# Per-sample 128x128 mix with residual: x loaded as 4096 B rows by channel instead of 8192 B rows, products over 128 rows instead of two groups of 64, weights loaded plain

## The reference, cut to what matters

```python
def reference(x, itok, weights):          # x [128, 128, 1024], itok [128], weights [8, 128, 128]
    w = weights[itok]                     # one 128x128 matrix per sample
    return x + einsum('bct,bcd->bdt', x, w)
```

## Time and profile before

| | before |
|---|---|
| median of 3 runs | 323.73 us |
| the profiled execution, its own time | 324.45 us |
| its span, first to last instruction | 322.8 us |
| mean granted TensorE clock | 0.929 of 2.4 GHz |
| PE, DVE, ACT, POOL busy | 76%, 50%, 41%, 17% |
| DMA | 134.80 MB, mean 418 GB/s |
| load queue (SP), store queue (ACT) | 49.9% and 49.2% of 16 engines' span |

### The profile page before, as it was taken

One profiled execution on the slowest core, in us unless ns is written; L12 is line 12 of the kernel. 1 busy time (PEld: TensorE's weight loads), 2 busy tenths in 40 slices (PEclk: granted clock), 3 DMA queues, 4 the chain that ended last, 5 costly groups with the idle time before them and its releaser, 6 DMA issues.

```text
span 322.8 us, 3365 instructions
## 1 busy us (share of the span) xinstructions
PE 243.8 (76%) x1088; PEld 110.6 (34%) x1088; DVE 160.5 (50%) x131; ACT 133.8 (41%) x132; POOL 55.1 (17%) x140
## 2 busy tenths in 40 slices
PE   3489999999978766888966687868798666878300
PEld 3334444444643322334322233323343222333100
DVE  0417677676674535452646643555536356435500
ACT  1015565566663424443534432434624244324300
POOL 5041222221221111110101111111101011100000
PEclk9879999999999998997999997989979999979855
DMA  7999999999999999999999999999999999999994
GB/s 289 425 420 420 404 429 424 426 428 425 427 428 426 428 427 428 429 425 429 427 427 427 428 427 426 429 426 427 428 426 428 428 426 427 428 426 428 427 428 208
DMA packets 17558, 134.80 MB, mean 418 GB/s; under 512 B 1041, under 2 KB 1042, under 8 KB 1170
## 3 DMA queue, kind: packets, MB, share of 16 engines
q1 hardware_dynamic: 8848, 67.64, 49.9%
q10 hardware_dynamic: 8706, 67.11, 49.2%
HBM read 67.63 MB, written 67.11 MB: 417 GB/s over the span
## 4 chain that ended last, share of the span: by engine, by line
DMA 60%; PE 27%; issue 2%; DVE 2%; POOL 1%; DVEq 1%; POOLq 0%; ACTq 0%; SPq 0%
DMA out<-ring 39%; PE products L170 25%; DMA ring<-x 21%; PE products L149 2%; DVE ring L198 1%; POOL pick L108 1%; DVEq L41 1%; DVE table L186 1%; POOL selected L133 0%; POOLq L128 0%; POOL ones L101 0%; DVE pick L182 0%; DVEq L193 0%; SPq L96 0%; ACTq L222 0%
## 5 line engine op out<-in xcount | busy, mean ns | idle before, releaser
L170 PE MATMUL products<-ring,selected 64*128 64x512 f32 x1024 | 237.2, 617 | 52.5 <-DMA ring<-x 46.6
L198 DVE COPY ring<-products 64x1024 f32<-64x1024 f32 x128 | 156.4, 1222 | 132.1 <-PE products L170 130.1
L214 ACT COPY ring<-products 64x1024 f32<-64x1024 f32 x128 | 128.7, 1006 | 163.3 <-PE products L170 161.6
L170 PEld LDWEIGHTS products<-ring,selected 64*128 64x128 f32 x1024 | 105.1, 195 | 184.3 <-issue 115.3
L133 POOL COPY selected<-table 64x256 f32 x128 | 50.7, 396 | 226.5 <-PE products L170 197.7
L149 PE MATMUL products<-loaded,pick 32*128 32x256 f32 x64 | 6.5, 588 | 4.9 <-DVE pick L182 4.9
L214 ACT ACT_TABLE_LOAD x4 | 5.1, 1283 | 6.0 <-DVE ring L198 2.9
L149 PEld LDWEIGHTS products<-loaded,pick 32*128 32x128 f32 x64 | 5.5, 310 | 5.5 <-POOL pick L108 4.8
L186 DVE TENSOR_TENSOR table<-products,unit 128x1024 f32<-128x1024 f32 x2 | 3.7, 1928 | 6.8 <-PE products L149 6.8
L108 POOL TENSOR_SCALAR_AFFINE_SELECT pick<-ones 32x512 f32<-32x512 f32 x4 | 2.6, 658 | 0.3
L182 DVE COPY pick<-pick 128x512 f32<-128x512 f32 x1 | 0.4, 426 | 4.3 <-POOL pick L108 4.3
## 6 DMA issues: line engine op xcount, KB each, us to landing
ring<-x SPq DMA_DIRECT2D x32, 2048.0 KB, 23.1
out<-ring ACTq DMA_DIRECT2D x32, 2048.0 KB, 43.7
loaded<-weights SPq DMA_DIRECT2D x1, 512.0 KB, 3.6
subject_row<-subjects ACTq DMA_DIRECT2D x1, 0.5 KB
```

Of the source, the lines that this page charges most:

```text
L170: last = nc.tensor.matmul(products[:, b, g, n * BANK:(n + 1) * BANK], selected[part, k, e * mixed:(e + 1) * mixed], ring[part, s, e * time ...
L198: nc.vector.tensor_copy(ring[0:HALF, s, b * times:(b + 1) * times], products[b * HALF:(b + 1) * HALF, s % PSUM_BUFS, 0, :]).then_inc(even_ ...
L214: nc.scalar.copy(ring[HALF:channels, s, b * times:(b + 1) * times], products[b * HALF:(b + 1) * HALF, s % PSUM_BUFS, 1, :]).then_inc(odd_d ...
```

## The change

Loads take x by channel: partition c holds channel c, with 4096 B (1024 times) of sample 0 and then of sample 1 of each tile. A span's load of 2 MB therefore is 128 partitions by four rows of 4096 B, where it was 128 by two rows of 8192 B; in x the four rows of a partition lie 512 KiB apart. Stores stay as they are. A product takes all 128 channels at once: 4 products of 128 rows by 512 columns per tile, without accumulation, where there were 8 of 64 rows. POOL still copies one matrix per sample, now on 128 partitions by 128 columns (64 by 256 before). The weights are loaded as eight 512 B rows per partition instead of one 4096 B row; `pick`, its doubling and the spreading products go away, and one DVE instruction adds the unit matrix straight to the loaded weights.

```diff
-    x_rows = x.rearrange("b (q e) t -> (b q) (e t)", e=2).rearrange("(t p) f -> p t f", p=channels)
+    x_rows = x.rearrange("b c t -> c b t")
...
-            sp.dma_start(loaded[:], weights.rearrange("n (h l) d -> (n h) (l d)", l=SIDE)).then_inc(weights_loaded, DMA)
+            sp.dma_start(loaded[:], weights.rearrange("n c d -> c n d")).then_inc(weights_loaded, DMA)
             for s in range(0, TILES_PER_TURN, SPAN):
-                sp.dma_start(ring[:, s:s + SPAN], x_rows[:, s:s + SPAN, :]).then_inc(x_loaded[s // SPAN], DMA)
+                sp.dma_start(ring[:, s:s + SPAN].rearrange("c s (g t) -> c (s g) t", g=2), x_rows[:, 2 * s:2 * (s + SPAN), :]).then_inc(x_loaded[s // SPAN], DMA)
...
-            for j in range(quarters):
...
-                nc.gpsimd.affine_select(pick[part, :, :, 0, :], ones[part, :], [[1, pairs], [-HALF, 2], [-1, HALF]],
-                                        ALU.is_equal, 0.0, base=0, channel_multiplier=4).then_inc(pick_ready, 1)
...
+            nc.gpsimd.affine_select(unit[:], ones[:], [[-1, mixed]],
+                                    ALU.is_equal, 0.0, base=0, channel_multiplier=1).then_inc(unit_ready, 1)
...
-                        nc.gpsimd.tensor_copy(selected[part, k:k + 1, :],
-                                              table[part, bass.ds(subject, 1), :]).then_inc(weights_selected[s], 1)
+                        nc.gpsimd.tensor_copy(selected[:, k, g:g + 1, :],
+                                              table[:, bass.ds(subject, 1), :]).then_inc(weights_selected[s], 1)
...
-            for n in range(2):
-                for r in range(pairs):
-                    for j in range(quarters):
...
-                        last = nc.tensor.matmul(
-                            weights_by_pair[:, at:at + wide],
-                            pick[part, r, n].rearrange("p g q -> p (g q)"),
-                            loaded[part, r * wide:(r + 1) * wide],
-                            start=(r == 0), stop=(r == pairs - 1))
...
-                    for n in range(banks):
-                        for e in range(2):
-                            for g in range(2):
...
-                                last = nc.tensor.matmul(
-                                    products[:, b, g, n * BANK:(n + 1) * BANK],
-                                    selected[part, k, e * mixed:(e + 1) * mixed],
-                                    ring[part, s, e * times + n * BANK:e * times + (n + 1) * BANK],
-                                    start=(e == 0), stop=(e == 1))
+                    for g in range(2):
...
+                        pe.wait_ge((even_drained, odd_drained)[g][last_user], 2 * turn + 2)
+                        for n in range(banks):
+                            last = nc.tensor.matmul(
+                                products[:, b, g, n * BANK:(n + 1) * BANK], selected[:, k, g, :],
+                                ring[:, s, g * times + n * BANK:g * times + (n + 1) * BANK],
+                                start=True, stop=True)
...
-            nc.vector.tensor_copy(pick[:, :, :, 1, :], pick[:, :, :, 0, :]).then_inc(pick_doubled, 1)
-            dve.wait_ge(unit_ready, 2)
-            dve.wait_ge(weights_spread, 1)
-            for e in range(2):
-                nc.vector.tensor_tensor(
...
+            dve.wait_ge(unit_ready, 1)
+            dve.wait_ge(weights_loaded, DMA)
+            nc.vector.tensor_tensor(
+                table[:].rearrange("p n (b m) -> p n m b", b=2),
+                loaded[:].rearrange("p n (m b) -> p n m b", b=2),
+                unit[:].rearrange("p (m b) -> p m b", b=2).unsqueeze(1).to_broadcast([channels, n_subjects, HALF, 2]),
+                ALU.add).then_inc(table_ready, 1)
```

More of the change, by code:

```diff
@@ L17 @@
 HALF = 64
-QUARTER = 32
-SIDE = 8
 def subject_mix_kernel(nc: bass.Bass, x: bass.AP, subjects: bass.AP, weights: bass.AP, out: bass.AP):
@@ L46, in subject_mix_kernel @@
         ring = ctx.enter_context(nc.sbuf_tensor("ring", [channels, TILES_PER_TURN, row], F32))
[L48 to L55, removed]
+        loaded = ctx.enter_context(nc.sbuf_tensor("loaded", [channels, n_subjects, mixed], F32))
+        table = ctx.enter_context(nc.sbuf_tensor("table", [channels, n_subjects, mixed], F32))
+        ones = ctx.enter_context(nc.sbuf_tensor("ones", [channels, mixed], F32))
+        unit = ctx.enter_context(nc.sbuf_tensor("unit", [channels, mixed], F32))
+        selected = ctx.enter_context(nc.sbuf_tensor("selected", [channels, SELECT_BUFS, 2, mixed], F32))
         subject_row = ctx.enter_context(nc.sbuf_tensor("subject_row", [1, samples], I32))
         products = ctx.enter_context(nc.psum_tensor("products", [mixed, PSUM_BUFS, 2, times], F32))
-        weights_by_pair = products[:, 0].rearrange("p g t -> p (g t)")
         subjects_loaded = sem("subjects_loaded")
@@ L95, in _ @@
                     sp.wait_ge(stored[s // SPAN], turn * DMA + DMA)
-                    sp.dma_start(ring[:, s:s + SPAN], x_rows[:, bass.ds(tile + TILES_PER_TURN, SPAN), :]
+                    sp.dma_start(ring[:, s:s + SPAN].rearrange("c s (g t) -> c (s g) t", g=2), x_rows[:, bass.ds(2 * tile + 2 * TILES_PER_TURN, 2 * SPAN), :]
                                  ).then_inc(x_loaded[s // SPAN], DMA)
@@ L102, in _ @@
             pool.wait_ge(ones_ready, 1)
-            for j in range(quarters):
-                part = slice(j * QUARTER, (j + 1) * QUARTER)
-                if j:
-                    pool.wait_ge(pick_ready, j)
-                nc.gpsimd.affine_select(pick[part, :, :, 0, :], ones[part, :], [[1, pairs], [-HALF, 2], [-1, HALF]],
-                                        ALU.is_equal, 0.0, base=0, channel_multiplier=4).then_inc(pick_ready, 1)
-            pool.wait_ge(pick_ready, quarters)
-            for g in range(2):
[L112 to L117, removed]
+            nc.gpsimd.affine_select(unit[:], ones[:], [[-1, mixed]],
+                                    ALU.is_equal, 0.0, base=0, channel_multiplier=1).then_inc(unit_ready, 1)
             pool.wait_ge(subjects_loaded, DMA)
-            pool.wait_ge(table_ready, 2)
+            pool.wait_ge(table_ready, 1)
             with pool.Fori(0, turns) as turn:
@@ L125, in _ @@
                     for g in range(2):
-                        part = slice(g * HALF, (g + 1) * HALF)
                         subject = pool.value_load(subject_row[0:1, bass.ds(2 * tile + g, 1)]).with_bounds(
@@ L139, in _ @@
                 pe.sem_inc(product_ready[s], 1)
-            pe.wait_ge(pick_ready, quarters)
-            pe.wait_ge(pick_doubled, 1)
-            pe.wait_ge(weights_loaded, DMA)
-            for n in range(2):
-                for r in range(pairs):
-                    for j in range(quarters):
-                        part = slice(j * QUARTER, (j + 1) * QUARTER)
-                        at = j * BANK + n * wide
-                        last = nc.tensor.matmul(
-                            weights_by_pair[:, at:at + wide],
-                            pick[part, r, n].rearrange("p g q -> p (g q)"),
-                            loaded[part, r * wide:(r + 1) * wide],
-                            start=(r == 0), stop=(r == pairs - 1))
-            last.then_inc(weights_spread, 1)
             with pe.Fori(0, turns) as turn:
@@ L180, in _ @@
                 dve.sem_inc(even_drained[s], 2)
-            dve.wait_ge(pick_ready, quarters)
-            nc.vector.tensor_copy(pick[:, :, :, 1, :], pick[:, :, :, 0, :]).then_inc(pick_doubled, 1)
-            dve.wait_ge(unit_ready, 2)
-            dve.wait_ge(weights_spread, 1)
-            for e in range(2):
-                nc.vector.tensor_tensor(
[L187 to L191, removed]
+            dve.wait_ge(unit_ready, 1)
[5 more added lines that the diff above has]
+                ALU.add).then_inc(table_ready, 1)
             with dve.Fori(0, turns) as turn:
```

7 lines of the change are left out of this document (removed).

## The result

The changed kernel takes 330.73 us (median of 4 runs, 329.85 to 334.93) against 323.79 us; the ratio is 1.0197, 95% interval 1.0177 to 1.0216. Six more runs of the same kernel, made later (experiment 6), gave 329.78 to 336.70 us, ratio 1.0252 (1.0206 to 1.0298): the kernel spreads by itself, and experiment 6 shows where. Each of the two ratios leaves out its slowest run, 334.93 and 336.70 us, as disturbed; whether it was, or had the late end of experiment 6, is not shown. The profiled execution took 330.01 us, its span is 328.3 us.

What follows compares the result with a forecast made beforehand. The prediction took the DMA engines, full from 5 to 318 us, as the bound. Packets 3.6, weights 0.4 and the end 6.0 made +10.0 us, 333.7 us against 323.73; own range 330.5 to 337, overall range 327.0 to 341.0.

Steps and rivals of the forecast that it cites:

- The bound: Whole kernel: bytes and packets over the DMA engines' rate, plus a start and a short end; PE has slack.
- Turns by packet: Engines alternate queues by packet, so stores get 283 GB/s, loads 141, and no line of stores forms; chance 0.60.
- The packets: Load queue: 8192 packets become 16384 of half size, +3.6 us; weights as 512 B rows, +0.4 us.
- the 7 ns for a packet: DMA engines: time a packet costs beside its bytes, giving +3.6 us for 8192 added load packets.
- The upper bound of 24.5 ns: Load packets: extra time per 8192 B, from the weights' 4096 B packets, making 12.5 us.
- The end: After the last load: 5.0 us of idle DMA plus 1.0 us for a lone store's start, +6.0 us.
- The sum: Whole kernel: +10.0 us on the profiled execution, median 333.7 us against 323.73.
- At no cost: Products at 7.14 us per span, copies, queues and waits: all taken as costing nothing.
- bytes: Rival at the DMA queues: turns by bytes keep the line of stores, only packets cost, 327.7 us; chance 0.20.
- pitch: Rival in the loads: rows 512 KiB apart in x read slower than their packets, 342.6 us; chance 0.11.
- PE: Rival in the products: unhidden weight loads make PE the bound, 10.1 us per span, about 342 us; chance 0.03.
- merged packets: Rival in the load queue: neighbouring 4096 B rows taken as one packet, not slower, 323.3 us; chance 0.06.

Runs made afterwards that it cites:

- experiment 6: The changed kernel, unchanged, run again: 333.66 us, ratio 1.0252; profiled execution 333.71 us.
- experiment 7: Changed kernel with PE held back until the third span of x has landed: 333.58 us, ratio 1.0254.
- experiment 9: Kernel before with half the ring, 8 tiles per turn instead of 16: 336.83 us, ratio 1.0406.
- Experiments 3: Kernel before with loads alone in 4096 B packets, both halves of a row in turn, one DMA per tile: 335.01 us, ratio 1.0296.
- experiment 4: Kernel before with stores alone in 4096 B packets, both halves of a row in turn: 326.08 us, ratio 1.0055.
- experiment 1: Changed kernel with its stores split too, so both queues move 4096 B packets: 328.26 us, ratio 1.0131.
- experiment 5: Loads and stores on one queue: changed kernel 328.19 us, ratio 1.0126; kernel before 325.64 us, ratio 1.0050.
- experiment 2: Kernel before, each load or each store split into two DMAs of half rows: loads 340.65 us, 1.0513; stores 341.48 us, 1.0533 (in the order told).

## Why the prediction was right, point by point

**The bound**, right: the DMA is full until 294 us in both kernels, and a PE that starts 7 us earlier gains nothing (in experiment 7 a start 10 us later costs nothing that shows), because the ring covers it (with half the ring, experiment 9, the start costs 8.4 us).

**Turns by packet**, right, and the heart of it: 430 packets against 431, a store landing in 11.8 us (about 10 was forecast). Experiments 3 and 4 turn it round by giving the same small packets to one queue or the other: +9.6 or +1.8 us. A load landed in 43.3 us, not 60.

**The packets** were the term that was mis-sized: 3.6 + 0.4 = 4.0 us, where the runs have 1.8 (experiment 4), 2.4 (from the rate in experiment 1) and 2.5 (the pair of experiment 5, with layout, weights and products in it). The failed step is the 7 ns for a packet, taken from a difference of record lengths in the earlier trace rows; both queues at 4096 B give 4.7 ns. The whole loss until 294 us is 3.2 us; of it 23 x (423 - 411)/428 = 0.6 us lie in the stretch from 5 to 28 us, in which loads run mostly alone. The upper bound of 24.5 ns from the earlier trace rows was, as suspected, a start-up stretch.

**The end** was forecast as 6.0 us and is two things: 2.3 us in the first profile, 6.0 us in that of experiment 6. The step that failed is "its own load landed one period earlier": in the first profile the last two loads landed 5.6 us apart. The loads do not land evenly. PE and ACT's queue from 62 us on show how they come:

```profile
65.54 23.54 PE L123 MATMUL products<-ring,selected 128*128 128x512 f32 x48 [4.21 <-DMA ring<-x]
91.73 8.66 PE L123 MATMUL products<-ring,selected 128*128 128x512 f32 x16 [2.66 <-DMA ring<-x]
...
78.08 0.38 ACTq L170 DMA_DIRECT2D out<-ring  x1
84.94 0.38 ACTq L170 DMA_DIRECT2D out<-ring  x1
91.81 0.38 ACTq L170 DMA_DIRECT2D out<-ring  x1
103.12 0.38 ACTq L170 DMA_DIRECT2D out<-ring  x1
```

48 instructions are three spans in one run. Their stores follow each other by 6.9 us, less than the 7.4 us that each was forecast to take beside loads, so loads crawl (1.73 MB in the 12 us shown above); then the stores run out, loads have the DMA alone, and the next spans land close together. Where the last span falls in such a group goes with the end: with its neighbour (2.3 us) or alone (6.0 us). That this grouping chooses the ending is read from profiles of both kinds, not forced by a run.

The rows of the two ends say more. In experiment 6 the last store is issued 3.7 us later (325.14 against 321.44). Of these 0.9 us are a later start of span 31 (305.59 against 304.71). Another 1.8 us are its products, 8.83 us against half of 14.00: PE had been without products for 4.19 us, and the granted clock from 306 to 312 us was 0.72 of 2.4 GHz, part of that time at the lower level of 1.2 GHz; in the first profile PE had paused for 0.54 us, and the clock was 1.00 from 304.7 to 311.7 us. A further 0.84 us are the wait for the last load's latest part. The prediction had slow first products only in its upper bound (1.4 us), and had nothing for a late part of a load. Where its 6.0 us agree with experiment 6, luck has a part: it had the DMA idle in one stretch, between the last two stores, and there it idles ahead of span 31's store as well. The 1.0 us for the start of a lone store was right: by the trace its first packet comes 0.9 us after its issue (321.44 and 322.35).

**The sum**: 333.7 us was forecast; 330.73 us in the first runs, 333.66 us in the second. The first lie 3 us below the forecast, near the lower end of its own range (330.5 to 337). That the second meet it within 0.1 us is partly luck: their profile has 3.2 us until 294 us, where 4.0 were forecast for the packets and the weights, and 6.0 us after it.

**At no cost**, right: a span's products take 7.1 us (14.0 for two) with 128 rows, weight loads hidden; POOL's copies 293 ns. SP is held, the median issue of a reload taking 9.9 us, and ACT's issues stay at 0.38 us. Of the rivals, bytes, pitch, PE and merged packets are each ruled out by a row above (430 packets against 431; 411 and 423 GB/s without the pitch; 66.1 us of PE idle, all for loads; 17936 packets of the load queue).

## What to carry to other kernels

Where two DMA queues share the engines, look at the packets each has, not at the bytes: a queue whose packets are made smaller falls behind, and the line of waiting work moves to its side. Ask on which side a line is useful: in front of the last stores it hides the last computation, in front of the loads it hides nothing at the end. If loads must have small rows, put loads and stores on one queue or give stores rows of the same size (328.2 and 328.3 us here, against 330.7 and 333.7), and keep the ring deep enough for the start.

## What the runs showed of the hardware that was not expected

- An added packet is cheap (4.7 ns, 2.4 us for 8192), but its queue's share is not: the same packets cost +1.8 us on the store queue and +9.6 us on the load queue.
- The parts of one DMA do not land together: half of the last load's marks were there by 307.8 and 307.9 us in the two profiles of the changed kernel, the last one at 310.3 and at 315.2.
- 4096 B loads alone run at 410 GB/s, beside stores both together at 427. All packets from 116 to 122 us in the changed kernel, loads only:

```profile
DMA packets 617, 2.46 MB, mean 410 GB/s; under 512 B 16, under 2 KB 16, under 8 KB 617
```

- Half rows: taking every other 4096 B in one DMA and the rest in the next costs 16 to 17 us (experiment 2), in stretches at 243 to 285 GB/s, when that queue works alone or nearly so. The same half rows for stores beside 4096 B loads cost nothing of the kind (experiment 1, 421 GB/s throughout). Why is open.
- One queue for both directions runs at 426 instead of 428 GB/s, and the kernel before loses 1.6 us by it.
